# Causal attention on one Trainium2 core: heads in the two row halves of the array, score banks in pairs, one pair of banks and one single bank for the maxima

## The chip, the core and the metric

The program runs on one core of a Trainium2 chip. The core has a matrix engine (TensorE, PE in the profile; its weight loads are PEld), VectorE (DVE), ScalarE (ACT), GpSimd (POOL) and SyncE (SP), which here only issues transfers. The engines run their own instruction streams in order and wait for each other through semaphores. PE reads SBUF and writes PSUM, which has 8 banks of 512 float32 columns on 128 partitions. The metric is the device time of the whole program in microseconds, as a median of several runs.

## The reference, cut to what matters

The program is a chain of eight sub-layers. Two of them are causal attention with 16 heads of 8 channels, on 4 sequences of 1024 tokens, and only those two are touched:

```python
q = q.reshape(B, T, n_head, D)            # B=4, T=1024, n_head=16, D=8
scores = jnp.einsum('bqhd,bkhd->bhqk', q, k) / jnp.sqrt(jnp.float32(D))
causal = jnp.tril(jnp.ones((T, T), dtype=bool))
scores = jnp.where(causal, scores, jnp.float32(-1e+30))
p = jax.nn.softmax(scores, axis=-1)
y = jnp.einsum('bhqk,bkhd->bqhd', p, v).reshape(B, T, C)
return y @ proj_w
```

Everything is float32 in the reference. The kernel keeps that precision for the scores with bfloat16 products: each of q and k is split into three bfloat16 parts, and six products of parts are summed.

## The kernel before

**Inputs.** `causal_inputs` (stage "ci", run as ci0 and ci1) projects eight chunks of 512 tokens, splits q and k into three bfloat16 parts with ACT and DVE, and SP stores the parts of each chunk into the DRAM tensors `q_parts` and `k_parts` (two transfers a chunk, `parts` is double buffered, so ACT waits for a chunk's store two chunks later).

**Attention.** `causal_attention` (stage "ca", run as ca0 and ca1) works on groups: a group G is four heads of one sequence, so there are 16 groups, four to a sequence ("batch"). For each group SP loads a *stack*: `queries` and `keys`, [128, 4 heads, 1024] in bfloat16. Rows 0 to 47 of a stack hold six copies of 8 channels (the six products), rows 64 and 65 hold the shift (minus the row maximum in two bfloat16 parts, against ones in `keys`), and the other rows are zero. Three stacks are used in turn (`RING_CA`). A stack needs 6 transfers for `queries`, 6 for `keys` (8 partitions x 4 heads x 1024 each) and one of zeros. At the start of the stage DVE clears the first stack, POOL the other two, and SP loads each when it is clear.

Two passes run over each group, interleaved:

- *Maxima* (`maximum`, PE L624 and the mask L627, DVE L783): queries against keys with the queries on the partitions, 128 rows by up to 512 keys, masked above the diagonal by a second matmul (identity times a mask), and DVE takes the maximum along the row. `MAXIMA` lists 20 tasks a group. Each task fills one pair of PSUM banks, and two pairs (banks 4-5 and 6-7) are used in turn: PE waits in `next_pair` for the task before the last to be reduced. When all maxima of a group are there, DVE makes the shift (`make_rows`, L792 to L794), PE turns it onto rows (`turn_rows`, L635, also in a pair of banks), ACT copies it out (`copy_rows`, L742) and SP places it into the stack (L564).
- *Scores* (`score`, PE L677 and the mask L680; ACT L759): keys on the partitions, up to 512 queries, for each of 12 units `(qc, kt)` and each of 4 heads one matmul into one of three single banks; ACT raises each bank by itself (exp) into `prob`. `weigh` (PE L691) multiplies `values` with `prob` in float32, four heads side by side in four column strips of 32, into bank 3. Diagonal units (kt >= 4 qc) are narrower (512, 384, 256, 128 columns) and masked: four with qc=0 and four of the eight with qc=1.

The order on PE is written out in the loop over units: score of heads 0 and 1, `between` slot 0, score of heads 2 and 3, `between` slot 1, then `weigh` of the unit before. `BETWEEN` says how many maxima tasks (of the next group) stand in each slot, `ROWS_UNIT` (8) the unit at which the rows are turned, and the tasks after it already belong to the group after the next.

**Batch ends.** When a sequence's four groups are done, `FINISH` puts its closing steps between the units of the next batch's first two groups: `totals` (PE L644: the softmax sums; DVE L800: reciprocal, and L92 to L96: split into bfloat16 parts), four `spread` (PE L654, DVE L809) and two `mix` (PE L662, float32 projection; DVE L819 or L821). The last batch's steps run alone at the end of the stage.

"Local attention" (L1100 to L1337) and the other stages are not touched. They make up the rest of the program.

## Time and profile before

| what | us |
|---|---|
| median of 3 runs | 6053.97 |
| lowest, highest | 6051.51, 6059.97 |
| the profiled execution, its own time | 6055.52 |
| its span, first to last instruction | 6053.7 |
| ca0: first clearing instruction to first matmul | 461.88 to 492.34 |
| ca0: first matmul of the maxima to the last output copy | 492.34 to 1123.4 |
| ca1: first clearing instruction to first matmul | 1686.95 to 1717.59 |
| ca1: first matmul of the maxima to the last output copy | 1717.59 to 2348.79 |

The two causal stages are a fifth of the time. A profile row of a timeline gives the start, the duration, the engine, the line, the operation, what it writes and reads, how many instructions are merged, and in brackets the idle time before it and who ended that. Matmuls are pipelined: a recorded matmul is longer than the time until the next can start, so the step from one start to the next is the price of one. A float32 matmul has two records. "128*32" is the part of the array (rows * columns) that a matmul uses.

### The profile page before, as it was taken

How to read it: one execution, taken by the hardware profiler on the slowest of the kernel's cores; microseconds unless marked ns; L12 is line 12 of the kernel's file. 1: busy time of each engine (PE TensorE's matmuls, PEld its weight loads, DVE VectorE, ACT ScalarE, POOL GpSimd, SP SyncE). 2: the span in 40 equal slices, each digit the busy share in tenths (PEclk: the TensorE clock that was granted, in tenths of full speed). 3: DMA queues.
4: the chain of work that ended last, by engine and by line, in shares of the span. 5: the costliest groups of instructions: out<-in, count | busy, mean ns of one | idle time of the engine just before them, and what ended most of it. 6: DMA issues, size and time to landing. Idle time of an engine off the chain costs nothing. (4 is left out here: it accounts for less than half of the span.)

```text
span 6053.7 us, 164948 instructions
## 1 busy us (share of the span) xinstructions
PE 5119.5 (85%) x72264; PEld 2980.0 (49%) x72592; DVE 4008.1 (66%) x4630; ACT 3245.7 (54%) x4392; POOL 1801.1 (30%) x1232
## 2 busy tenths in 40 slices
PE   6756999788769996998799979997999799979997
PEld 3422333333323332666366636663666366636663
DVE  5756666233366664887488748884888488848884
ACT  2323555322235554776377637763777367736773
POOL 0003000000030001555155515551555055505550
PEclk9988999899889998999899989998999899989998
DMA  0011110000011111111111111110111011101111
GB/s 24 0 48 33 23 23 18 21 0 0 29 39 23 24 21 38 38 38 34 34 39 39 34 33 38 38 38 32 38 38 38 30 37 38 39 31 37 37 37 40
DMA packets 87157, 186.93 MB, mean 31 GB/s; under 512 B 23216, under 2 KB 39088, under 8 KB 84272
## 3 DMA queue, kind: packets, MB, share of 16 engines
q1 hardware_dynamic: 86448, 176.44, 12.1%
q8 instruction: 572, 9.37, 0.6%
q14 instruction: 137, 1.12, 0.1%
HBM read 59.97 MB, written 14.68 MB: 12 GB/s over the span
## 5 line engine op out<-in xcount | busy, mean ns | idle before, releaser
L1327 POOL TENSOR_TENSOR part_of_local<-part_of_local,sine_of_local 128x512 f32<-128x512 f32 x768 | 960.2, 1273 | 1061.3 <-DVE sine_of_local L1264 1061.3
L783 DVE TENSOR_REDUCE top_of_ca<-ps 128x2 f32<-128x1024 f32 (+3 forms) x640 | 695.1, 1115 | 298.6 <-PE ps L627 207.2
L759 ACT ACTIVATE prob_of_ca<-ps 128x512 f32<-128x512 f32 (+3 forms) x1536 | 654.5, 495 | 422.6 <-PE ps L680 311.0
L1334 POOL TENSOR_TENSOR part_of_local<-part_of_local,inverse_of_local 128x1024 f32<-128x1024 f32 x384 | 722.5, 1903 | 139.7 <-DVE inverse_of_local L1296 139.7
L624 PE MATMUL ps<-keys_of_ca,queries_of_ca 128*128 128x512 bf16 (+3 forms) x1474 | 386.4, 332 | 180.6 <-DMA queries_of_ca<-zeros_of_ca 86.4
L1301 DVE TENSOR_REDUCE total_of_local<-prob_of_local 128x16 f32<-128x1024 f32 x192 | 234.3, 1220 | 421.2 <-ACT prob_of_local L1240 421.2
L1261 DVE TENSOR_TENSOR part_of_local<-ps,rope 128x1024 f32<-128x1024 f32 x384 | 466.2, 1214 | 40.7 <-ACT square_of_local L1208 40.7
L1264 DVE TENSOR_TENSOR sine_of_local<-ps,rope 128x1024 f32<-128x1024 f32 x384 | 465.7, 1213 | 0.0
L1100 PE MATMUL ps<-qkv,shifted 128*128 128x512 f32 x768 | 392.4, 635 | 82.1 <-POOL values_of_local L1337 78.5
L1110 PE MATMUL ps<-qkv,shifted 128*128 128x512 f32 x768 | 381.6, 620 | 84.9 <-ACT heads_out_of_local L1236 71.8
L677 PE MATMUL ps<-queries_of_ca,keys_of_ca 128*128 128x512 bf16 (+2 forms) x1464 | 404.0, 331 | 24.3 <-issue 10.8
L1186 PEld LDWEIGHTS ps<-prob_t_of_local,mixed_of_local 64*64 64x64 f32 x12288 | 335.0, 135 | 166.2 <-issue 156.7
L1195 PE MATMUL ps<-heads_out_of_local,wo 128*128 128x128 f32 x3072 | 387.6, 281 | 14.1 <-ACT heads_out_of_local L1236 13.7
L1186 PE MATMUL ps<-prob_t_of_local,mixed_of_local 64*64 64x32 f32 x12288 | 383.8, 221 | 16.0 <-issue 9.1
L1186 PE MATMUL ps<-prob_t_of_local,values_of_local 64*64 64x32 f32 x12288 | 382.0, 219 | 4.7 <-issue 4.2
L1195 PEld LDWEIGHTS ps<-heads_out_of_local,wo 128*128 128x128 f32 x3072 | 368.8, 197 | 16.8 <-ACT heads_out_of_local L1236 16.7
L1167 PE MATMUL ps<-qkv,shifted 128*64 128x512 f32 x1536 | 376.9, 607 | 0.1
L594 POOL MEMSET queries_of_ca<- 32x4096 bf16 x12 | 42.1, 3505 | 1106.1 <-POOLq L63 1105.5
L1226 ACT ACTIVATE keys_of_local<-ps 128x1024 f32<-128x1024 f32 x192 | 196.8, 1025 | 323.2 <-PE ps L1129 323.2
L1247 ACT ACTIVATE values_of_local<-ps 128x1024 f32<-128x1024 f32 x192 | 196.6, 1024 | 306.2 <-PE ps L1167 306.2
L1186 PEld LDWEIGHTS ps<-prob_t_of_local,values_of_local 64*64 64x64 f32 x12288 | 338.0, 135 | 6.8 <-issue 5.9
L691 PE MATMUL ps<-prob_of_ca,values_of_ca 128*32 128x512 f32 (+3 forms) x3072 | 332.5, 505 | 0.0
(207 smaller groups left out, 9928.3 us busy)
## 6 DMA issues: line engine op xcount, KB each, us to landing
mixed_of_local<-values_of_local SPq DMA_DIRECT2D x636, 128.0 KB, 2.4
mixed_of_local<-values_of_local SPq DMA_DIRECT2D x264, 64.0 KB, 2.0
queries_of_ca<-q_parts SPq DMA_DIRECT2D x192, 64.0 KB
keys_of_ca<-k_parts SPq DMA_DIRECT2D x192, 64.0 KB
qkv<-in_qkv SPq DMA_DIRECT2D x7, 1536.0 KB, 6.5
rope<-in_rope SPq DMA_DIRECT2D x7, 1024.0 KB, 9.0
q_parts<-parts_of_ci SPq DMA_DIRECT2D x16, 384.0 KB, 2.5
k_parts<-parts_of_ci SPq DMA_DIRECT2D x16, 384.0 KB, 2.5
```

The lines of the kernel that those rows point to most:

```text
L624: last = nc.tensor.matmul(to[:, h, :], queries[:, first + h, qt * P:(qt + 1) * P], keys[:, first + h, lo:lo + width], start=True, stop=not ...
L677: last = nc.tensor.matmul(to, keys[:, h, kt * P:(kt + 1) * P], queries[:, h, qc * CH + j:(qc + 1) * CH], start=True, stop=not diagonal)
L759: nc.scalar.activation(prob[:, i % 2, h, j:], ps[:, n % SCORE_BANKS, j:], ACT.Exp, scale=scale).then_inc(raised, 1)
L783: nc.vector.reduce_max(top[:, slot, first:first + heads], in_pair(n, heads, width), AX_X)\
L1100: last = nc.tensor.matmul(two_banks(SCORE_SLOT)[:, a, :], xs[:, tokens(t)], w["qkv"][:, 0, chunk(a)], start=True, stop=True)
L1110: last = nc.tensor.matmul(two_banks(KEY_SLOT)[:, a, :], xs[:, tokens(t)], w["qkv"][:, 1, chunk(a)], start=True, stop=True)
L1186: last = nc.tensor.matmul(out, src[rows, t % RING * 2 + i // 2, p + e, :], prob_t[rows, p + e, i * WIN:(i + 1) * WIN], start=True, stop=True)
L1195: last = nc.tensor.matmul(two_banks(OUT_SLOT)[:, 0, 0:P], w["o"][:, p, :], heads_out[:, p, :], start=p == 0, stop=p == PAIRS - 1)
L1261: nc.vector.tensor_tensor(part[:, t % 2, side], by_head(slot), table(2 * side, t), ALU.mult).then_inc(parts, 1)
L1264: nc.vector.tensor_tensor(sine[:, side], by_head(slot), table(2 * side + 1, t), ALU.mult).then_inc(parts, 1)
L1327: nc.gpsimd.tensor_tensor(out, out, sine[:, side, :, (1 - to) * half:(2 - to) * half], ALU.add).then_inc(rotated, 1)
L1334: nc.gpsimd.tensor_tensor(part[:, t % 2, side], part[:, t % 2, side], by, ALU.mult).then_inc(scaled, 1)
```

## The change

The two causal stages only. Constants first: `SHIFT_ROW` goes from 64 to 32, `ROW_HALF` = 64 is new.

- A stack becomes [128, 2, 1024]: of a pair of heads the even one lies in rows 0 to 63 and the odd one in rows 64 to 127 (channels in rows 0-31 and 34-49 of a half, shift in rows 32 and 33, zeros behind). Loads are 12 transfers for `queries`, 12 for `keys` (8 partitions x 2 x 1024) and 2 of zeros, 26 instead of 13.
- The stacks are allocated outside of the stage, cleared by POOL during "ci" (19 chained memsets) and the first three are loaded by SP during "ci", each behind the stores of chunks 3, 4 and 5; "ci" ends when they have landed.
- `score` fills two banks (0-1 or 2-3) with two matmuls of 64 rows each, one in each row half, then the two masks (128 rows). ACT raises two banks with one instruction. The sum bank is 4.
- `maximum`: the 48 pieces (12 strips x 4 heads) are cut into 14 tasks of 4 or 2 pieces in one pair of banks (5-6) and 12 tasks of one piece in a single bank (7), alternating; 26 tasks instead of 20. PE waits for the pair's last task before it fills the pair again, and likewise for the single bank.
- `copy_rows` on ACT moves from within unit 9 to right behind the second exp of unit 8.
- Batch ends: ACT copies the totals out of PSUM, the reciprocal is two halves of 256 columns, the split is two steps, and all steps are spread over units of three groups (11 places instead of 7).

```diff
-MAXIMA = [(qt, lo, width, h, heads, slot) for qt in range(TILES)
-          for lo, width, slot in ([(0, CH, qt)] if qt >= 4 else []) +
-          [(qt // 4 * CH, (qt % 4 + 1) * P, qt + qt // 4 * 4)]
-          for heads in (HG if width <= 2 * P else 2,) for h in range(0, HG, heads)]
+STREAM = [3 * n + 12 for n in range(7)]
+MAXIMA = in_turn([(0, 4), (4, 4), (8, 2)] + [(q, 2) for q in STREAM] + [(32, 4), (36, 4), (40, 2), (44, 2)],
+                 [(10, 1), (11, 1)] + [(q + 2, 1) for q in STREAM[:6]] + [(42, 1), (43, 1), (46, 1), (47, 1)])
-BETWEEN = ((1, 1), (1, 1), (1, 0), (1, 0), (1, 1), (1, 1), (1, 1), (1, 1), (1, 1), (1, 1), (1, 0), (1, 0))
+BETWEEN = ((2, 1), (1, 1), (1, 0), (1, 0), (2, 1), (2, 1), (2, 1), (2, 1), (2, 1), (1, 1), (1, 0), (1, 0))
-FINISH = {(0, 4): ("totals", 0), (0, 6): ("spread", 0), (0, 7): ("spread", 1), (0, 10): ("mix", 0),
-          (1, 4): ("spread", 2), (1, 5): ("spread", 3), (1, 8): ("mix", 1)}
+FINISH = {(0, 4): ("totals", 0), (0, 5): ("invert", 0), (0, 6): ("invert", 1), (0, 7): ("split", 0), (0, 8): ("split", 1),
+          (1, 4): ("spread", 0), (1, 6): ("spread", 1), (1, 8): ("mix", 0),
+          (2, 4): ("spread", 2), (2, 6): ("spread", 3), (2, 8): ("mix", 1)}
...
+                    for low in range(0, pieces, 2):
+                        for n in range(low, min(low + 2, pieces)):
+                            slot, h = divmod(first + n, HG)
+                            qt, lo, width = strip(slot)
+                            diagonal, half = lo + width == (qt + 1) * P, slice(ROW_HALF * (h % 2), ROW_HALF * (h % 2 + 1))
+                            last = nc.tensor.matmul(place_of(n, pieces, width), queries[half, h // 2, qt * P:(qt + 1) * P],
+                                                    keys[half, h // 2, lo:lo + width], start=True, stop=not diagonal)
...
-                        if n >= SCORE_BANKS:
-                            pe.wait_ge(raised, n - SCORE_BANKS + 1)
...
+                    if n >= 2:
+                        pe.wait_ge(raised, n - 1)
+                    for e in range(2):
+                        half = slice(ROW_HALF * e, ROW_HALF * (e + 1))
+                        last = nc.tensor.matmul(ps[:, 2 * two + e, j:], keys[half, two, kt * P:(kt + 1) * P],
+                                                queries[half, two, qc * CH + j:(qc + 1) * CH], start=True, stop=not diagonal)
+                    if diagonal:
+                        for e in range(2):
+                            last = nc.tensor.matmul(ps[:, 2 * two + e, j:j + P], k["ident_b"][:, :], k["after_k"][:, :],
+                                                    start=False, stop=True)
...
-                            nc.scalar.activation(prob[:, i % 2, h, j:], ps[:, n % SCORE_BANKS, j:], ACT.Exp,
-                                                 scale=scale).then_inc(raised, 1)
+                            nc.scalar.activation(prob[:, i % 2, 2 * two:2 * two + 2, j:], ps[:, 2 * two:2 * two + 2, j:],
+                                                 ACT.Exp, scale=scale).then_inc(raised, 1)
...
+                    if 3 <= c < 3 + RING_CA:
+                        if c == 3:
+                            sp.wait_ge(cleared, 1 + 6 * RING_CA)
+                            for slot in range(4):
+                                sp.wait_ge(stored[slot], 16)
+                        load_stack(sp, fetched[c - 3], stacks, zeros, q_parts, k_parts, c - 3)
```

**PE, unit 8 of a group** (the diagonal unit at which the rows are turned; L677, L680 and L691 become L737, L741 and L753, and L624, L627 and L635 become L676, L681 and L689). Before, from the last two scores on:

```order
L677 MATMUL ps<-queries_of_ca,keys_of_ca 128x512
L680 MATMUL ps<-sb_after_k,sb_ident_b 128x128
L677 MATMUL ps<-queries_of_ca,keys_of_ca 128x512
L680 MATMUL ps<-sb_after_k,sb_ident_b 128x128
L635 MATMUL ps<-sb_ident_b,neg_parts_of_ca 8x128 x8
L624 MATMUL ps<-keys_of_ca,queries_of_ca 128x256
L627 MATMUL ps<-sb_after_q,sb_ident_b 128x128
L624 MATMUL ps<-keys_of_ca,queries_of_ca 128x256
```

And after, the whole unit up to its `weigh`:

```order
L737 MATMUL ps<-queries_of_ca,keys_of_ca 128x512 x2
L741 MATMUL ps<-sb_after_k,sb_ident_b 128x128 x2
L676 MATMUL ps<-keys_of_ca,queries_of_ca 128x128 x2
L681 MATMUL ps<-sb_after_q,sb_ident_b 128x128 x2
L676 MATMUL ps<-keys_of_ca,queries_of_ca 128x128 x2
L681 MATMUL ps<-sb_after_q,sb_ident_b 128x128 x2
L676 MATMUL ps<-keys_of_ca,queries_of_ca 128x384
L681 MATMUL ps<-sb_after_q,sb_ident_b 128x128
L737 MATMUL ps<-queries_of_ca,keys_of_ca 128x512 x2
L741 MATMUL ps<-sb_after_k,sb_ident_b 128x128 x2
L689 MATMUL ps<-sb_ident_b,neg_parts_of_ca 8x128 x8
L676 MATMUL ps<-keys_of_ca,queries_of_ca 128x256 x2
```

The matmuls of a pair now stand together, with 64 rows each, and their masks, with 128 rows, behind them; so the part of the array in use changes at each line of the second list. The task behind the turned rows now needs the same pair of banks as these.

**DVE, first group of a batch, units 5 to 8.** Before, the closing steps of the last batch stand in two blocks (the reciprocal and its split at unit 4, a spread at unit 6):

```order
L783 TENSOR_REDUCE top_of_ca<-ps 128x4
L800 RECIPROCAL inverse_of_ca<-ps 128x512
L92 CAST inverse_parts_of_ca<-inverse_of_ca 128x512
L93 SCALAR_TENSOR_TENSOR inverse_of_ca<-inverse_parts_of_ca,sb_minus_first,inverse_of_ca 128x512
L95 CAST inverse_parts_of_ca<-inverse_of_ca 128x512
L96 SCALAR_TENSOR_TENSOR inverse_parts_of_ca<-inverse_parts_of_ca,sb_minus_second,inverse_of_ca 128x512
L783 TENSOR_REDUCE top_of_ca<-ps 128x2 x4
L809 TENSOR_TENSOR evened_of_ca<-summed_of_ca,ps 128x1024
```

After, maxima of pairs (L852, L854) and of single banks (L846) stand between the pieces:

```order
L872 RECIPROCAL inverse_of_ca<-inverse_of_ca 128x256
L846 TENSOR_REDUCE top_of_ca<-ps 128x1
L852 TENSOR_REDUCE top_of_ca<-ps 128x2
L846 TENSOR_REDUCE top_of_ca<-ps 128x1
L872 RECIPROCAL inverse_of_ca<-inverse_of_ca 128x256
L854 TENSOR_REDUCE top_of_ca<-ps 128x2x2
L846 TENSOR_REDUCE top_of_ca<-ps 128x1
L854 TENSOR_REDUCE top_of_ca<-ps 128x2x2
L879 CAST inverse_parts_of_ca<-inverse_of_ca 128x512
L881 SCALAR_TENSOR_TENSOR inverse_of_ca<-inverse_parts_of_ca,sb_minus_first,inverse_of_ca 128x512
L846 TENSOR_REDUCE top_of_ca<-ps 128x1
```

No block of closing steps is left that holds DVE for more than one of them.

**SP, end of "ci".** After, with the stores of chunks 3 to 6:

```order
L505 DMA k_parts<-parts_of_ci 128x3x512
L403 DMA queries_of_ca<-q_parts 8x2x1024 x12
L403 DMA keys_of_ca<-k_parts 8x2x1024 x12
L405 DMA queries_of_ca<-zeros_of_ca 2x2x1024 x2
L505 DMA q_parts<-parts_of_ci 128x3x512
L505 DMA k_parts<-parts_of_ci 128x3x512
L403 DMA queries_of_ca<-q_parts 8x2x1024 x12
```

Before, the stores of all chunks stood in a row there, and the loads stood in "ca" behind the clearing.

## Rows read from the trace of the kernel before

**Rows 1.** The page's head, and its busy time by engine.
```profile
span 6053.7 us, 164948 instructions
...
PE 5119.5 (85%) x72264; PEld 2980.0 (49%) x72592; DVE 4008.1 (66%) x4630; ACT 3245.7 (54%) x4392; POOL 1801.1 (30%) x1232
```

**Rows 2.** Windows: stretch, length, busy (count) by engine, clock, DMA share, GB/s.
```profile
462.00:492.30 30.30, 0.00 (x0) 0.00 (x0) 14.55 (x8) 0.00 (x0) 29.84 (x9) 0.50 0.19 32
...
523.60:1140.00 616.40, 540.49 (x4204) 232.21 (x4271) 377.80 (x385) 355.46 (x816) 5.64 (x14) 0.96 0.12 24
...
1686.00:1717.00 31.00, 0.00 (x0) 0.00 (x0) 14.55 (x8) 0.00 (x0) 29.59 (x9) 0.50 0.18 29
```

**Rows 3.** Windows: a group in the middle, then a batch's first two.
```profile
591.83:624.07 32.24, 30.48 (x261) 13.77 (x264) 22.33 (x24) 22.09 (x52) 0.40 (x1) 1.00 0.16 27
...
656.31:703.87 47.56, 39.95 (x288) 16.34 (x292) 31.27 (x32) 22.67 (x52) 0.40 (x1) 0.93 0.11 18
703.87:742.08 38.21, 35.30 (x273) 15.43 (x276) 25.38 (x27) 22.50 (x52) 0.41 (x2) 1.00 0.13 23
```

**Rows 4.** Timeline, PE and ACT, units 6 to 9 of that group.
```profile
605.47 1.06 PE L691 MATMUL ps<-prob_of_ca,values_of_ca 128*32 128x512 f32 x8
...
607.88 0.38 PE L624 MATMUL ps<-keys_of_ca,queries_of_ca 128*128 128x512 bf16 x1
608.10 0.22 PE L627 MATMUL ps<-sb_after_q,sb_ident_b 128*128 128x128 bf16 x1
608.15 0.38 PE L624 MATMUL ps<-keys_of_ca,queries_of_ca 128*128 128x512 bf16 x1
608.37 0.22 PE L627 MATMUL ps<-sb_after_q,sb_ident_b 128*128 128x128 bf16 x1
608.52 1.07 PE L691 MATMUL ps<-prob_of_ca,values_of_ca 128*32 128x512 f32 x8
609.52 0.39 PE L677 MATMUL ps<-queries_of_ca,keys_of_ca 128*128 128x512 bf16 x1
...
614.27 1.00 ACT L742 ACTIVATE rows_of_ca<-ps 8x1024 bf16<-8x1024 f32 x1
615.33 0.34 PE L624 MATMUL ps<-keys_of_ca,queries_of_ca 128*128 128x384 bf16 x1 [1.26 <-ACT rows_of_ca L742]
```

**Rows 5.** Timeline, PE in local attention, where row halves are used.
```profile
3004.44 2.00 PE L1156 MATMUL ps<-keys_of_local,queries_of_local 64*32 64x64 f32 x128
3006.37 1.94 PE L1167 MATMUL ps<-qkv,shifted 128*64 128x512 f32 x8
```

**Rows 6.** Groups by line and shape: count, busy us, mean ns, idle before.
```profile
L783 DVE TENSOR_REDUCE top_of_ca<-ps 128x2 f32<-128x1024 f32 x384 | 457.4, 1221 | 142.0 <-PE ps L624 81.5 <-PE ps L627 56.0
L759 ACT ACTIVATE prob_of_ca<-ps 128x512 f32<-128x512 f32 x768 | 402.4, 604 | 204.2 <-PE ps L680 101.1 <-PE ps L677 69.0 <-remote 34.0
...
L783 DVE TENSOR_REDUCE top_of_ca<-ps 128x4 f32<-128x512 f32 x64 | 44.2, 691 | 30.0 <-PE ps L627 27.3 <-DVE neg_parts_of_ca L794 0.3
```

**Rows 7.** The page's group of an ACT instruction over two banks.
```profile
L1226 ACT ACTIVATE keys_of_local<-ps 128x1024 f32<-128x1024 f32 x192 | 196.8, 1025 | 323.2 <-PE ps L1129 323.2
```

**Rows 8.** Timeline, the starts of ca0 and ca1.
```profile
461.88 3.50 POOL L594 MEMSET queries_of_ca<- 32x4096 bf16 x1 [461.42 <-POOLq L63]
...
480.43 2.04 SPq L556 DMA_DIRECT2D queries_of_ca<-q_parts  x6
...
492.34 0.29 PE L624 MATMUL ps<-keys_of_ca,queries_of_ca 128*128 128x128 bf16 x1 [44.69 <-DMA queries_of_ca<-zeros_of_ca]
...
1683.49 0.36 SPq L469 DMA_DIRECT2D k_parts<-parts_of_ci  x1
...
1717.59 0.29 PE L624 MATMUL ps<-keys_of_ca,queries_of_ca 128*128 128x128 bf16 x1 [41.70 <-DMA queries_of_ca<-zeros_of_ca]
```

**Rows 9.** Timeline, DVE in a batch end and at ca1's end.
```profile
665.36 3.36 DVE L800 RECIPROCAL inverse_of_ca<-ps 128x512 f32<-128x512 f32 x1 [1.99 <-PE ps L644]
...
2330.71 2.59 DVE L809 TENSOR_TENSOR evened_of_ca<-summed_of_ca,ps 128x1024 f32<-128x1024 f32 x2 [1.25 <-PE ps L654]
```

More of the change, by code:

```diff
@@ L629, in maximum @@
-                    last.then_inc(ready, 1)
+                    if i == 0 and G >= RING_CA:
+                        pe.wait_ge(loaded[G % RING_CA], STACK_LOADS * (G // RING_CA))
+                    if pieces > 1:
+                        take_pair()
+                    else:
+                        take_lone()
+                    for low in range(0, pieces, 2):
[5 more added lines that the diff above has]
+                                                    keys[half, h // 2, lo:lo + width], start=True, stop=not diagonal)
+                        for n in range(low, min(low + 2, pieces)):
+                            qt, lo, width = strip((first + n) // HG)
+                            if lo + width == (qt + 1) * P:
+                                last = nc.tensor.matmul(place_of(n, pieces, width)[:, width - P:], k["ident_b"][:, :],
+                                                        k["after_q"][:, :], start=False, stop=True)
@@ L667, in score, with finish @@
+                def finish(b, step, which):
+                    if step == "totals":
+                        totals(b)
+                    elif step == "spread":
+                        spread(b, which)
+                    elif step == "mix":
+                        mix(b, which)
+                def score(G, i, two):
                     qc, kt, j = UNITS[i]
                     queries, keys = stacks[G % RING_CA]
-                    diagonal = kt >= 4 * qc
-                    if i == 0 and heads[0] == 0:
+                    diagonal, n = kt >= 4 * qc, 2 * (G * NU + i) + two
+                    if i == 0 and two == 0:
@@ L717, in _ @@
                     G, i = divmod(u, NU)
-                    score(G, i, (0, 1))
-                    between(G, i, 0)
-                    score(G, i, (2, 3))
-                    between(G, i, 1)
+                    for two in range(2):
+                        score(G, i, two)
+                        between(G, i, two)
                     if u:
@@ L771, in _ @@
                 sum_out(ALL - 1, 1)
+                take_totals(lones)
                 act.wait_ge(acc_out, 2 * ALL)
@@ L850, in _ @@
                 maximum(NM)
-                next(task)
+                next(pairs)
                 for m in range(NM + 1, NM + AHEAD):
```

349 lines of the change are left out of this document (184 added, 165 removed).

## The prediction, made before the changed kernel ran

> **What bounds the kernel now.** I read the page's head first: the span is 6053.7 us, and PE is the busiest engine at 85% of it [rows 1]. Only the two causal stages change, so I went on to windows over them [rows 2]. Each has a start in which PE does nothing at all (30.3 us in ca0, 31.0 in ca1: DVE and POOL clear stacks, then a load lands) and a long body in which PE is busy 540 of 616 us. The body repeats itself, so I took one group of it: 32.24 us, PE 30.48 busy, DVE 22.33, ACT 22.09, clock 1.00 [rows 3]. PE bounds the group. The two other windows there are the groups that carry a batch end: 47.56 and 38.21 us, so a batch end costs 15.3 + 6.0 = 21.3 us, part of it at a lower clock (0.93).
>
> Then I priced PE by the steps between starts [rows 4]. A 512-column bfloat16 matmul takes 607.88 to 608.10, 0.216 us. Its 128-column mask takes 608.10 to 608.15, 0.055. The float32 weighing begins 0.15 behind the last mask (608.37 to 608.52) and the next score starts 1.00 behind it (608.52 to 609.52); streaming is 2048 column passes at 2.4 GHz, 0.85. So going from the full array to 32-column strips costs about 0.095 beyond the matmul itself, and going back about as much again. The unit 605.47 to 608.52 checks these prices: 1.00 + 0.095 + 8 x 0.216 + 4 x 0.055 = 3.04 against 3.05 measured. By them a group is 9.4 us of scores (18,432 columns and 32 masks), 9.4 of maxima, 7.7 of weighing, 0.45 of turned rows and 26 changes of array shape at 0.095 (2.5): 29.5, and with small overheads 29.8. The other 2.4 us are waits, 1.26 of them one wait for ACT's copy of the rows.
>
> **The change, part by part. (a) The start.** The clearing and the first load leave the stage: 461.9 to 492.3 in ca0 and 1687.0 to 1717.6 in ca1 [rows 8], 30.4 + 30.6 = 61.0 us. They go under "ci", where POOL is idle; its 3.50 us memset of 32x4096 halves with its size, so 19 chained ones take about 33 us. SP gets three loads of 26 transfers: at 2.04 us for six [rows 8] one load takes 26 x 0.34 = 8.8 us to issue, ahead of the next chunk's stores. The first load of before (13 transfers, the same bytes) was ready 11.9 us after its first issue (480.43 to 492.34); twice as many, half as long transfers may take between that and twice that. In ci0 three loads from about 420 on end near 462, when the stage ends anyway: 0 to 4 us lost, I take 2. In ci1 the stage is shorter: clearing ends near 1661, the loads follow, the stores of chunks 4 and 5 stand behind them, ACT waits for these two chunks later, and the stage then ends 9 to 20 us behind its last store of before (1683.5), I take 14, nearer to the load's measured 11.9. Net: -61 + 16 = -45 us.
>
> **(b) PE's work in a group.** If the two halves of a pair run side by side, a score pair costs 0.216 instead of 0.43: -3.8 us. Of the 48 maxima pieces 36 are paired and 12 stand alone, so their columns fall from 18,432 to 12,032: -2.7. Masks stay. Against that, a pair uses 64 rows, its mask 128, the weighing 32-column strips: I counted 88 changes of shape in the order of a group where there were 26. The trace has no change between the full array and full-width halves. The nearest rows are those in [rows 4] and one in local attention, where 64*32 matmuls give way to 128*64 ones: all are about 0.095. I take that: 62 x 0.095 = +5.9. The bounds are 0 and, for a full pipeline, 0.16 (0.38 recorded against 0.216 stepped). PE's work is then 29.8 - 6.5 + 5.9 = 29.2 us, hardly less than before. That halves overlap isn't proved by the trace: the 128 records of L1156 in eight array parts take 1.93 us (3004.44 to 3006.37) [rows 5], against 6.8 us one after the other, but 1.7 us if only the four column strips overlapped. So a pair costs between 0.22 and 0.43, and I take 0.22, since column strips do overlap (8 records of mean 605 ns in 1.06 us).
>
> The Trainium skill, "TensorE: Matmul & The Clock Gate", section "Packing small matmuls", says that matmuls in different row groups run concurrently (four of 32 rows 3.07 times as fast); [rows 5] doesn't contradict it. The skill's "TensorEngine Tiling (Array Packing)", "Key Properties", says that changing the tiling mode drains the array. That speaks against this change, and the 0.095 in [rows 4] agrees. By the first page alone the body would gain 6.5 us a group, 28 x 6.5 = 182 us.
>
> **(c) The waits in a group.** Times by [rows 6] and [rows 7]: a reduction of 1024 columns 1.22 us, of 512 0.69; exp over two banks 1.03 instead of 2 x 0.60; the rows' copy 1.00; a release reaches PE 0.06 later (615.27 to 615.33), a result its reader about 0.2 after the last start. DVE's sum grows by six instructions of 0.16 to 23.3, ACT's falls to about 20. Neither is the bound over a group, but both are over parts of it. I walked through the group in PE's order, from unit 4, where three maxima tasks (2, 1, 2 banks) stand in each unit:
> - unit 4: DVE has 3.1 us of work, PE 1.5. PE fills the pair, the single bank, scores, then must wait until the first pair is reduced: 1.0 us.
> - unit 5: the same for its pair: 0.6.
> - unit 6: 0.1.
> - unit 7: two pair tasks follow each other, with a 0.96 us reduction between: 1.0.
> - unit 8: turned rows and the next task use the same pair. ACT first ends the second exp of the unit (1.03), then copies (1.00): 1.65 against 1.26 + 0.2 before. Queued behind this wait on PE are the weighing of unit 7 and all of unit 9.
> - the rest: 0.1. Here PE is the bound with 15.7 us up to the next unit 4.
> Together 4.5 us, so a group takes 29.2 + 4.5 = 33.7 us against 32.24: +1.45. For 14 groups of each stage: 28 x 1.45 = +41 us.
>
> **(d) The last two groups** of a stage have few or no maxima. There the exps over two banks leave fewer waits between ACT and PE: -4.5 a stage, -9.
>
> **(e) Batch ends.** The first group pays 1.9 for totals on PE and the rest by DVE's 3.4 us of reciprocal [rows 9] and 2.4 of split in units where DVE is already late: 5.5. The next two pay a spread twice (2.1 each) and a float32 mix of 3.5 on PE less some overlap: 7.3 each. Sum 20.1 against 21.3: six batch ends, -7. The serial end of a stage gets a copy of the totals (0.6 and a handover) and no longer fills the second pair while DVE reads the first (2.59 for two in a row [rows 9]): +2.5 a stage, +5.
>
> **Sum:** -45 + 41 - 9 - 7 + 5 = -15 us. The profiled execution took 6055.52 (span 6053.7 and 1.8 around it), so it would become 6040.5; the median of before is 1.55 lower, so the median of after is about **6039 us**, 0.25% less.
>
> **Rivals.**
> - *Change of shape is cheap* between full array and row halves (0 to 0.03 us). PE's work falls to about 24.7, DVE holds units 4 to 7 (12.4 us), the rest shrinks by some 4: about 30 us a group, 28 x -3.7 = -104: near 5935. For it: no row shows this very change. Against: every other change of shape that I found costs the same. The page's promise of twice the speed for pairs is this case.
> - *Slower: the hand-over of the single pair is the bound.* In each group five waits of PE (c) end on one reduction or copy, where before two pairs took turns and PE could be a task ahead. If each is 0.3 us longer than my walk, or the loads of 26 transfers come late for the group after the next, a group is 35.2: +42, near 6081. It decides against the kernel from 34.2 us a group on (28 x 0.5 = 14 more uses up the gain). For it: DVE's work in units 4 to 7 is already 10.9 us against PE's 10.3.
> - *The halves don't overlap* (the change doesn't do what it says): PE's work +6.5, of which perhaps 5 shows: 28 x 5 = +140, near 6179.
> - *The loads choke "ci":* transfers at half the rate, stores queued behind: 22 us more, near 6061.
> - *The walk is too strict* by 0.8 us a group, since tasks of both kinds can run ahead a little: -22, near 6017.
>
> **How the numbers follow.** Forecast 0.50 (own range 6020 to 6060), cheap change 0.10, slower by the hand-over 0.18, no overlap 0.06, loads 0.05, walk too strict 0.11. The range leaves out the cheap change, no overlap and the far ends of the others: 5990 to 6095. A measurement of this kernel can tell 0.2%, 12 us, from no change, so faster means below 6042 and slower above 6066: faster 0.10 + 0.11 + 0.28 of the forecast's half = 0.49; same 0.17 + 0.03 = 0.20; slower 0.31.
>
> **What the profile of after would show.** (a) The first matmul of ca0 within 1 us of the stage's start, the end of ci1 later by some 14 us than its last store before. (b) In a diagonal score 0.31 us from the first L737 to the first L741, and two L737 starts a few ns apart; with 0.22 the cheap change holds, with 0.5 there is no overlap. (c) POOL's copies of values 33.7 us apart in the middle of a batch; waits of PE's L676 on DVE and on ACT's copy of the rows of about 4.5 us a group. (e) About 20 us more in three groups of a batch, at clock 1.00. I am wrong if the distance in the middle of a batch is under 33 or over 34.5 us.

## The result, and the profile of the changed kernel

The changed kernel takes **6147.7 us** (median of four runs, 6133 to 6152), the kernel before beside it 6054.0. The ratio is 1.0142, with a 95% interval of 1.0123 to 1.0160: slower by some 86 us by the ratio, and 94 between the two medians. The forecast was 6039 with a range of 5990 to 6095, so both the sign and the range were wrong.

The page's head and windows over the changed kernel answer to [rows 1] and [rows 3]. The columns of a window are as in [rows 2]: stretch, length, busy time of PE, PEld, DVE, ACT and POOL, clock, DMA share, GB/s.

```profile
span 6147.5 us, 164154 instructions
...
PE 5202.0 (85%) x72386; PEld 2892.2 (47%) x72592; DVE 4000.2 (65%) x4814; ACT 3214.3 (52%) x3632; POOL 1770.4 (29%) x1242
```
```profile
465.67:546.14 80.47, 65.46 (x397) 20.13 (x397) 53.43 (x67) 24.79 (x30) 2.30 (x4) 0.69 0.01 4
...
580.79:616.85 36.06, 32.51 (x266) 10.80 (x264) 22.92 (x30) 21.01 (x28) 0.40 (x2) 0.95 0.10 26
...
616.85:651.50 34.65, 31.11 (x266) 10.70 (x264) 22.93 (x30) 21.02 (x28) 0.41 (x2) 1.00 0.09 24
651.50:692.87 41.37, 34.81 (x282) 11.24 (x280) 28.20 (x36) 21.84 (x29) 0.40 (x2) 0.96 0.08 21
692.87:736.66 43.79, 37.39 (x277) 12.48 (x276) 26.05 (x33) 21.12 (x28) 0.40 (x2) 0.96 0.08 19
736.66:780.40 43.74, 37.30 (x277) 12.48 (x276) 26.05 (x33) 21.11 (x28) 0.40 (x1) 0.96 0.07 20
856.45:904.03 47.58, 41.25 (x277) 12.77 (x276) 26.12 (x33) 21.12 (x28) 0.40 (x2) 0.86 0.07 18
```

The first row is the prologue (maxima of group 0, PE's work ahead of the first score) with group 0 in ca0, from the first matmul on. The third row is a quiet group: 34.65 us, where [rows 3] has 32.24 and the forecast 33.7. The second is the same group with its clock at half speed (1.2 instead of 2.4 GHz) for a part. The next three are one batch end in three groups, each with such a fall (0.96), and the last is one of them where the clock fell longer.

Added up over the two stages, from one profiled execution each (6149.3 against 6055.5 us):

| stretch | forecast | measured |
|---|---|---|
| (a) both starts, "ci" with them | -45 | -46.6 |
| prologue and group 0, both stages | +3 (as two groups) | +27.1 |
| (b, c) 26 quiet groups, 34.65 - 32.24 each | +38 | +62.7 |
| (e) six batch ends, 20.4 at full clock against 21.3 | -7 | -5 |
| falls to half clock inside the groups | 0 | +46 |
| (d) last two groups of a stage | -9 | -8 |
| serial ends | +5 | +3 |
| stages that the change doesn't touch | 0 | +15 |

A fall costs 1.4 us or more: 36.06 - 34.65. What the batch ends take without it is read below from "full_rows", where some stand at clock 1.00. The falls are what is left of 98.5 us, by which both stages grew behind group 0, when the rows for quiet groups, batch ends, last groups and serial ends are taken off. The last row can't be called an effect of the change: between profiled executions these stages differ that much with the same code. Behind ca1 the kernel before takes 3705.6 us and the changed kernel 3717.9, but of the kernels below "early_before" takes 3729.1, "own_masks_three" 3721.0 and "filled_prologue" 3704.4.

**The start** did what the sum said. Timeline of the changed kernel, PE in both stages and SP at the end of "ci1":

```profile
465.67 0.29 PE L676 MATMUL ps<-keys_of_ca,queries_of_ca 64*128 64x128 bf16 x2 [14.11 <-PEq L65]
...
1690.55 4.04 SPq L403 DMA_DIRECT2D queries_of_ca<-q_parts  x12
1694.63 4.05 SPq L403 DMA_DIRECT2D keys_of_ca<-k_parts  x12
1698.73 1.41 SPq L405 DMA_DIRECT2D queries_of_ca<-zeros_of_ca  x2
...
1724.90 1.10 SPq L505 DMA_DIRECT2D k_parts<-parts_of_ci  x1
...
1730.41 0.29 PE L676 MATMUL ps<-keys_of_ca,queries_of_ca 64*128 64x128 bf16 x2 [20.26 <-PEq L65]
```

This load holds SP for 9.6 us (1690.55 to 1700.14, estimated 8.8), the next two for 10.5 each. The stores of the next chunk stand behind each of them. From the first matmul of "ci1" to the start of ca1 it now takes 14.5 us longer (estimated 14), and in "ci0" the same time as before. So the two idle starts of 61.1 us less 14.5 give the 46.6.

**The quiet group.** Its timeline on PE, units 4, 5, 7 and 8:

```profile
624.53 0.39 PE L676 MATMUL ps<-keys_of_ca,queries_of_ca 64*128 64x512 bf16 x2 [0.89 <-DVE top_of_ca L852]
...
626.26 0.39 PE L676 MATMUL ps<-keys_of_ca,queries_of_ca 64*128 64x512 bf16 x2 [0.34 <-DVE top_of_ca L852]
...
634.25 0.39 PE L676 MATMUL ps<-keys_of_ca,queries_of_ca 64*128 64x512 bf16 x2 [0.84 <-DVE top_of_ca L852]
...
635.79 0.39 PE L737 MATMUL ps<-queries_of_ca,keys_of_ca 64*128 64x512 bf16 x2
636.11 0.28 PE L741 MATMUL ps<-sb_after_k,sb_ident_b 128*128 128x128 bf16 x2
636.33 0.23 PE L676 MATMUL ps<-keys_of_ca,queries_of_ca 64*128 64x128 bf16 x2
...
640.13 0.28 PE L676 MATMUL ps<-keys_of_ca,queries_of_ca 64*128 64x256 bf16 x2 [1.47 <-ACT rows_of_ca L787]
```

The four waits of the walk are all there, in the units it named: 0.89, 0.34, 0.84, 1.47 against 1.0, 0.6, 1.0, 1.65. And a score pair gives way to its mask after 0.32 us (635.79 to 636.11): 0.216 for two matmuls side by side and 0.10 for the change of shape. Overlap and price were right. What was wrong is found below.

### The profile page after: what moved, and what is told of

Same layout as the page of the kernel before. It is cut to its first block and busy times, and to the rows that moved or that the text cites. A ratio compares the mean times of both kernels' runs of the same rounds, so it can differ in the third digit from the quotient of the medians.

```text
span 6147.5 us, 164154 instructions
## 1 busy us (share of the span) xinstructions
PE 5202.0 (85%) x72386; PEld 2892.2 (47%) x72592; DVE 4000.2 (65%) x4814; ACT 3214.3 (52%) x3632; POOL 1770.4 (29%) x1242
## 5 line engine op out<-in xcount | busy, mean ns | idle before, releaser
L814 ACT ACTIVATE prob_of_ca<-ps 128x1024 f32<-128x1024 f32 (+3 forms) x768 | 615.7, 812 | 564.1 <-PE ps L741 394.4
L676 PE MATMUL ps<-keys_of_ca,queries_of_ca 64*128 64x512 bf16 (+3 forms) x1536 | 342.3, 355 | 201.6 <-DVE top_of_ca L852 77.4
L852 DVE TENSOR_REDUCE top_of_ca<-ps 128x2 f32<-128x1024 f32 (+1 forms) x320 | 374.0, 1169 | 140.0 <-PE ps L681 84.8
L1275 PE MATMUL ps<-heads_out_of_local,wo 128*128 128x128 f32 x3072 | 388.9, 281 | 13.8 <-ACT heads_out_of_local L1316 13.5
L637 POOL COPY values_of_ca<-vtok 128x256 f32<-128x256 f32 x32 | 12.7, 402 | 1200.8 <-PE ps L753 1200.7
L753 PE MATMUL ps<-prob_of_ca,values_of_ca 128*32 128x512 f32 (+3 forms) x3072 | 355.1, 536 | 0.4 <-ACT summed_of_ca L800 0.4
L1327 ACT ACTIVATE values_of_local<-ps 128x1024 f32<-128x1024 f32 x192 | 196.6, 1024 | 303.4 <-PE ps L1247 303.4
L846 DVE TENSOR_REDUCE top_of_ca<-ps 128x1 f32<-128x512 f32 (+1 forms) x384 | 245.8, 640 | 132.5 <-PE ps L681 97.3
```

Of the source, the lines that this page charges most:

```text
L753: last = nc.tensor.matmul(ps[h * QUAD:(h + 1) * QUAD, SUM_BANK, j:], values[:, G % 2, kt, h, :], prob[:, i % 2, h, j:], start=kt == 0, sto ...
L814: nc.scalar.activation(prob[:, i % 2, 2 * two:2 * two + 2, j:], ps[:, 2 * two:2 * two + 2, j:], ACT.Exp, scale=scale).then_inc(raised, 1)
L852: nc.vector.reduce_max(to, pair[:, :, 0:width], AX_X).then_inc(pair_used, 1)
L1275: last = nc.tensor.matmul(two_banks(OUT_SLOT)[:, 0, 0:P], w["o"][:, p, :], heads_out[:, p, :], start=p == 0, stop=p == PAIRS - 1)
```

## The experiments

Ratios are to the kernel before, run on the same chip. In all, the question is which of four things made the groups and the prologue longer: the changes of shape, the row halves themselves, the changed banks and order, or the clock.

**1. The early loads alone.** First the kernel before, with its stacks of 128 rows, cleared and loaded early (cut to the lines that matter):

```
-                sp.wait_ge(first_cleared, 8)
-                load(0)
+    (in "ci", behind the stores of chunks 3, 4, 5)
+                        load_stack(sp, fetched[c - 3], stacks, zeros, q_parts, k_parts, c - 3)
```

> The kernel before with one part of the change alone: the stacks (still one of 128 rows with four heads, 13 transfers a load) are cleared by POOL in the stages ahead and the first three loads go out under "ci". Theory (step (a) of the prediction is right, and the cold prologue of the changed kernel comes from its row halves): the first matmul of ca0 and ca1 comes 27 to 30 us sooner, the clock rises some 5 us behind the first matmul as in the kernel before, the first group ends 67 us behind the first matmul as before: 45 to 55 us less than before, about 6003. Rival (the clock stays low because PE starts right behind the stage "ci"): the prologues take about 80 us instead of 67, and only 20 to 28 us are gained, about 6030. In both the distance in the middle of a batch stays 32.24.

Measured: 0.9985 (0.9974 to 0.9996). Neither theory had it: the memsets for two stacks were longer than the layernorm that I had put them under, and "ci0" began 29 us late. That is a fault of the experiment, mended in the next.

> As "early_before", but the clearing no longer fills the layernorms ahead: there one stack is cleared (24.5 us), under "ci" two, two loads go out under "ci" and the third in the attention stage. In "early_before" the stage "ci0" began at 410.9 instead of 381.6 us and ca0's first matmul stood where it had stood before, since 49 us of memsets are longer than a layernorm. Theory (step (a) holds for the full array): "ci0" begins within 3 us of before, both stages' first matmuls come 25 to 30 us sooner, "ci1" ends 0 to 8 us later than before; in all 45 to 55 us less than before. Rival (the early loads cost under "ci" or in the prologue what they save): less than 20 us.

Measured: **0.9925** (0.9900 to 0.9950), 46 us less. The first matmuls come 30.3 us (ca0) and, from the start of "ci1", 28.7 us (ca1) sooner, and the distance in the middle stays 32.24. Step (a) is confirmed apart from the rest. With the loads of the changed kernel put back into the attention stages:

> The changed kernel with clearing and the first three loads back in the attention stages. Theory (row halves keep the clock low whatever came before; step (a) of the prediction holds): PE's first matmul comes about 24 us behind the stage's start, "ci1" ends 13 us sooner, the prologue stays at clock 0.50 for its whole length: 25 to 35 us slower than the changed kernel. Rival (the clock stayed low because the start was early): the prologue is at full clock 5 us behind the first matmul and 13 us shorter in each stage, so that the time is within 10 us of the changed kernel.

Measured: 1.0194 (1.0177 to 1.0212), 31 us slower than the changed kernel, as the theory said. The prologue of ca0 takes 79.06 us at a mean clock of 0.71; it was 80.47 at 0.69 in the changed kernel. That isn't the 0.50 throughout that I had expected, but it shows that the early start doesn't cause the slow prologue.

**2. Without the changes of shape.** Each mask now goes into its head's row half, by two matmuls of 64 rows; constants with swapped halves are added (put in short, as it is for the even head):

```
-  nc.tensor.matmul(to, k["ident_b"][:, :], k["after_k"][:, :], start=False, stop=True)
+  own = slice(ROW_HALF * e, ROW_HALF * (e + 1))
+  nc.tensor.matmul(to[:, low], k["ident_b"][own, :], k["after_k"][own, low], start=False, stop=False)
+  nc.tensor.matmul(to[:, high], k["ident_r"][own, :], k["after_k_r"][own, high], start=False, stop=True)
```

> The changed kernel, but each causal mask is added by two matmuls of 64 rows in the half of its head (the constants stand a second time with their halves swapped; 128 and 64 columns), so that scores, maxima and masks have one shape and only weighing and turned rows change it: 26 changes of shape a group instead of 88. Theory (a change of shape costs 0.095 us on PE and PE bounds much of the group): 5.9 us less PE work; part of it turns into waits for DVE in units 4 to 7, so the quiet group falls from 34.65 to 30.5 to 31.5 us and the whole by 85 to 120 us, to 6030 to 6060. Rival (the hand-over of the single pair is the bound, changes of shape lie beside it): the group stays above 33.8 and the whole falls by less than 25 us.

Measured: **0.9853** (0.9836 to 0.9869), 175 us less than the changed kernel, more than I had expected. The quiet group:

```profile
595.14:624.49 29.35, 25.01 (x330) 10.71 (x328) 22.79 (x30) 20.45 (x28) 0.41 (x2) 1.00 0.10 29
```

62 changes of shape fewer (26 instead of 88) take 5.3 us off a group, 0.085 each: most of their 0.10 lay on the path. The rest of the gain is in prologue and batch ends, and in the falls of the clock: no quiet group of this kernel shows one.

**3. Without the overlap.** Both heads of a pair use row half 0, so the second head gets the wrong rows:

> The changed kernel, but both heads of a pair use the first row half (the second head reads the first one's rows, so its results are the wrong head's): same instructions, shapes and banks, no overlap. Theory 1 (the halves do run side by side): PE's work in a group rises by 3.8 us of scores and 2.7 of maxima, the quiet group from 34.65 to 39 to 41 us, the whole by 110 to 170 us. Theory 2 on the clock (it stays low in the prologue because of how long PE works, not because of the rows used): the prologue's matmuls now keep PE busy twice as long and the clock rises within 20 us as in the kernel before. Rival to 2 (64 rows are too few whatever the time): it stays at 0.50 for the whole prologue, which gets longer still.

Measured: 1.1488 (1.1454 to 1.1522). One pair at full clock, then a quiet group:

```profile
722.93 0.60 PE L737 MATMUL ps<-queries_of_ca,keys_of_ca 64*128 64x512 bf16 x2
723.47 0.28 PE L741 MATMUL ps<-sb_after_k,sb_ident_b 128*128 128x128 bf16 x2
```
```profile
576.34:642.19 65.85, 64.62 (x265) 15.74 (x264) 23.69 (x30) 21.56 (x28) 0.40 (x2) 0.50 0.05 12
```

The pair takes 0.54 instead of 0.32 us, so the halves of the changed kernel do run side by side. But the group was not 39 to 41 us. The clock is 0.50 for the whole prologue of ca0 (116 us) and 0.56 on average over the 554 us behind it; in the group shown it stays at half speed while PE is busy for 64.6 of 65.9 us. My theory on the clock falls, its rival holds.

**4. The waits for DVE, and the batch ends.** DVE's maxima over half the columns of each piece; and the changed kernel without the batch ends inside the stages:

> The changed kernel with each of DVE's maxima taken over half the columns of its piece (the shift is then only a part's maximum). Theory (2.1 us of a quiet group are waits of PE for DVE through the single pair of banks, the rest is PE's own work and the copy of the rows): the quiet group falls from 34.65 to 32.3 to 32.8 us, batch ends by as much, the whole by 55 to 75 us. Rival (DVE is the bound over a longer stretch, PE only seems busy): the group falls below 31.5. Other rival (the waits move to ACT's exp): above 34.

> The changed kernel without the batch ends inside the two stages: the totals, inverses, spreading and mixing of the first three batches are left out, only the last batch's at the stage's end are made. Theory (a batch end costs 25 us at full clock, and the waits in it bring most of the clock falls): six batch ends, 150 us, and 10 to 20 us of falls go: 150 to 175 us less than the changed kernel. Rival (the falls come from the quiet groups' own waits and changes of shape): only 140 to 150 us, and 3.4 us at half clock still stand in every second or third group. By step (e) of the prediction it would be 120.

Windows of quiet groups, one of "half_reduce", then one of "no_batch_ends":

```profile
531.83:566.34 34.51, 32.35 (x266) 10.81 (x264) 13.96 (x30) 20.77 (x28) 0.40 (x1) 0.95 0.09 24
```
```profile
549.04:586.46 37.42, 33.87 (x266) 10.89 (x264) 22.92 (x30) 20.99 (x28) 0.40 (x1) 0.91 0.07 21
```

"half_reduce": 0.9996 (0.9984 to 1.0009), 88 us less than the changed kernel. The waits for DVE in a group fell from 2.1 to 0.7 us, yet the group stayed at 34.5. Every one now had a part at half clock (0.95), and a fall costs the 1.4 us that the waits had given back. The theory (32.3 to 32.8) missed this, and so did the rival that named 34, since no wait for an exp appeared. The gain came from batch ends and prologues. The prologue of ca0 shows DVE's share in it, at a clock as low as the changed kernel's:

```profile
460.55:531.83 71.28, 64.25 (x397) 19.96 (x397) 32.54 (x68) 24.56 (x30) 2.30 (x5) 0.70 0.02 4
```

"no_batch_ends": 0.9879 (0.9856 to 0.9901), 159 us less. That is the 120 us by which step (e) had it, and falls of the clock: 26 groups now take 14 us more than 26 x 34.65, where some 46 had been lost. So my 25 us a batch end were 20 of work and 5 of clock, and falls stay in groups without any batch end, up to 37.42 us, as the rival said.

**5. Full rows in the changed order.** The changed kernel's banks, tasks, exps and batch ends, but stacks of 128 rows (and the third load in the attention stage):

```
-  queries[half, h // 2, qt * P:(qt + 1) * P], keys[half, h // 2, lo:lo + width]
+  queries[:, h, qt * P:(qt + 1) * P], keys[:, h, lo:lo + width]
```

> The changed kernel with its order of tasks, its pair and single bank, its exps over two banks, its spread batch ends and early loads (two under "ci", the third in the attention stage), but with stacks of 128 rows and four heads, loads of 13 transfers, as in the kernel before: no row halves. Theory (the row halves are what costs: 61 changes of shape a group and a clock that 64-row matmuls do not raise): the prologue to the end of the first group takes 64 to 68 us instead of 80, the clock falls go, the quiet group is 32 to 33 us, and the whole is 6000 to 6035. Rival (the hand-over through one pair and one single bank is what costs): the quiet group stays above 34 us and the whole above 6060.

Measured: 1.0076 (1.0055 to 1.0097), 6102 us. My theory falls. Its quiet group, its first batch end with the first group of the next, and PE's waits in the quiet group show why:

```profile
582.60:617.06 34.46, 31.32 (x265) 14.16 (x264) 23.03 (x30) 21.03 (x28) 0.40 (x1) 1.00 0.16 25
```
```profile
651.52:691.35 39.83, 33.63 (x281) 14.34 (x280) 28.31 (x36) 21.75 (x29) 0.41 (x2) 1.00 0.13 21
691.35:733.73 42.38, 36.12 (x277) 15.88 (x276) 26.16 (x33) 21.03 (x28) 0.41 (x2) 1.00 0.13 21
733.73:776.11 42.38, 36.12 (x277) 15.88 (x276) 26.16 (x33) 21.03 (x28) 0.40 (x2) 1.00 0.12 20
810.57:851.91 41.34, 35.14 (x281) 14.71 (x280) 28.29 (x36) 21.74 (x29) 0.40 (x1) 0.96 0.13 20
```
```profile
PE ps L678 <- DVE top_of_ca L854: 1.7, 3, 0.8
PE ps L678 <- ACT rows_of_ca L789: 1.3, 1, 1.3
```

The group is 2.2 us longer than before with the same matmuls: three new waits of PE for DVE through the single pair of banks. A batch end at clock 1.00 is 5.4 + 7.9 + 7.9 = 21.2 us here, and one fall to 0.96 costs 1.5 (41.34 against 39.83). Taking that 1.5 off the changed kernel's 41.37, 43.79 and 43.74 leaves 5.2 + 7.6 + 7.6 = 20.4. "late_loads", whose groups have the changed kernel's code, has one such group at clock 1.00, the second of a batch end's three. It is 7.7 above 34.65:

```profile
1037.58:1079.94 42.36, 35.92 (x277) 12.40 (x276) 26.06 (x33) 21.12 (x28) 0.41 (x2) 1.00 0.06 16
```

The cross test keeps the row halves and goes back to the banks, order and batch ends of before:

> The kernel before's banks and order (two pairs of banks for maxima in turn, three single score banks, one exp a head, its batch ends), with the change's row halves (masks in the full array as in the change) and early loads. Theory (the row halves are nearly even, -6.5 for overlap and +6 for changes of shape, and the single pair of the change costs its 2.2 us a group): the quiet group is 31.4 to 32.3 us, 2.3 to 3.2 below the change's 34.65, and the whole 5985 to 6020, near "early_before_two". Rival (row halves need the change's order, since a pair of scores now waits for two of three banks): above 33.5. For the clock: if 64-row matmuls keep it low, the prologue shows 45 us or more at half clock as in the change; if the gaps of the single pair do, 20 us or less, as in the kernel before.

> "two_pairs_full_masks" with each mask in the row half of its head, as in "own_half_masks": before's banks and order, row halves, 26 changes of shape a group. Theory (with changes of shape and hand-over both gone, PE's own work of 24.1 us and the 1.5 us wait for the rows remain, and ACT's 22.1 and DVE's 22.3 us come close): quiet group 26 to 28.5 us, the whole 5840 to 5900, below every kernel so far. Rival (ACT becomes the bound, since 48 exps of one bank each wait for scores that come in pairs): quiet group 29 us or more, no better than "own_masks_three".

Measured: 1.0015 (1.0003 to 1.0026) and **0.9828** (0.9811 to 0.9845). Neither side of the first expectation had it: its group takes 33.35 us, between 32.3 and 33.5. Windows of prologue with group 0, and of a quiet group, for "early_before_two", "full_rows" (prologue), "two_pairs_full_masks" and "halves_two_pairs":

```profile
462.07:525.91 63.84, 51.89 (x391) 23.58 (x398) 50.94 (x54) 25.98 (x57) 2.30 (x4) 0.96 0.11 17
558.15:590.39 32.24, 30.48 (x261) 13.77 (x264) 22.34 (x24) 22.08 (x52) 0.41 (x2) 1.00 0.17 26
```
```profile
468.41:548.14 79.73, 61.94 (x396) 27.45 (x397) 53.18 (x67) 24.59 (x30) 2.30 (x5) 0.75 0.08 14
```
```profile
461.64:530.96 69.32, 59.73 (x398) 18.73 (x398) 51.98 (x54) 26.07 (x56) 2.30 (x5) 0.72 0.05 16
530.96:564.31 33.35, 30.94 (x266) 10.52 (x264) 22.55 (x24) 22.26 (x52) 0.40 (x2) 1.00 0.09 25
```
```profile
466.62:527.93 61.31, 48.39 (x513) 20.37 (x514) 51.35 (x54) 25.92 (x56) 2.29 (x4) 0.73 0.07 18
527.93:557.70 29.77, 25.80 (x329) 10.60 (x330) 22.32 (x24) 22.27 (x52) 0.40 (x2) 1.00 0.09 28
```

Together they make a table of the quiet group (in brackets prologue with group 0, ca0):

| | banks and order of before | of the change |
|---|---|---|
| full rows | 32.24 (63.8) | 34.46 (79.7) |
| row halves, masks full | 33.35 (69.3) | 34.65 (80.5) |
| row halves, masks in them | 29.77 (61.3) | 29.35 (69.4) |

Read down, row halves cost a group 1.1 us or next to nothing while the masks change the shape, and save 2.5 to 5.1 when they don't. Read across, the changed banks and order cost 2.2 us with full rows, 1.3 with row halves, and nothing in the last line. The effects don't add up: "halves_two_pairs" got 29.77 instead of 26 to 28.5, because scores now wait for ACT's exps, as its rival had said (PE's waits, over 557.70 to 587.59):

```profile
PE ps L719 <- ACT prob_of_ca L806: 2.3, 7, 0.6
PE ps L662 <- ACT rows_of_ca L789: 1.5, 1, 1.5
```

In the prologue the changed banks and order cost 16, 11 and 8 us, the lower clock that came with them included.

**6. The clock in the prologue.** Full-array matmuls of no use behind each of the 33 tasks ahead of the first score (the expectation says 31); they write a score bank:

> The changed kernel with two more matmuls of the full array (512 columns, bfloat16, result not used) behind each of the 31 tasks of maxima ahead of the first score. Theory (the clock stays at half speed for 58 us because 64-row matmuls with gaps keep too little of the array at work, and this costs the prologue 13 us): the clock is full within 10 us, and first matmul to end of the first group falls from 80 to about 70 us in both stages: 15 to 25 us less in all. Rival (something else holds the clock down): it stays at 0.50, the 62 matmuls cost 0.43 us each, and the time rises by 20 to 50 us.

Measured: 1.0104 (1.0087 to 1.0121), 23 us less than the changed kernel. That is the expected size, but by luck. The clock does come up (window over prologue and group 0 of ca1, below; 0.86 in ca0), yet the window shrinks from 81.2 to 75.2 in ca1 and from 80.5 to 79.9 in ca0: 6.5 us of the 27, with the time of the added matmuls in it. The two profiled executions are 14.1 us apart, and 13.5 of them lie behind ca1, in stages that the edit doesn't touch. So 6.5 us is what this experiment shows.

```profile
1743.48:1818.69 75.21, 68.77 (x459) 22.46 (x463) 52.88 (x67) 24.62 (x30) 2.30 (x5) 0.95 0.02 4
```

**7. A version that beats both.** "own_half_masks" with four more edits, in three steps. First the third load goes out in the attention stage and the spreading moves, then one task of maxima moves, last the prologue is filled. The two tables, in short:

```
-  (2, 1), (2, 1), (2, 1), (2, 1), (2, 1), (1, 1), (1, 0), (1, 0))      tasks between scores, units 4 to 11
+  (2, 1), (2, 1), (2, 1), (2, 1), (2, 0), (2, 1), (1, 0), (1, 0))
-  (1, 4): ("spread", 0), (1, 6): ("spread", 1)        first slot of the unit
+  (1, 2): ("spread", 0), (1, 3): ("spread", 1)        second slot
```

> "own_half_masks" with two more edits: the third load goes out in the attention stage instead of under "ci", and in a batch end the two pairs of totals are spread in the second slot of units 2 and 3, where no task of maxima follows at once. Theory: "ci1" ends 7 to 10 us sooner; of the 2.6 us that PE waits for the spreading in each of two groups of a batch end, 1.5 to 2.5 go, 12 such groups, 18 to 30 us: in all 25 to 40 us less than "own_half_masks". Rival (the spreading holds up the tasks behind it wherever it stands, since DVE's work is the same): only the 7 to 10 us of the load.

> "own_masks_two" with one task of maxima moved from behind the turned rows in unit 8 to unit 9, so that PE does not need the pair of banks while ACT ends an exp and copies the rows (1.1 to 1.5 us in each group). Theory: that wait goes in 30 groups, 25 to 40 us less than "own_masks_two". Rival (the tasks behind it are late by as much, since DVE and the single pair are the bound there): less than 10 us.

> "own_masks_three" with one more full-array matmul of 512 columns (result not used) behind each of the 31 tasks of maxima ahead of the first score. Theory (64-row matmuls alone do not raise the clock, full-array ones do): the time at half clock in the prologue falls from about 50 to below 20 us and each prologue becomes 4 to 7 us shorter: 8 to 14 us less. Rival: the clock rises, but the added matmuls cost what it gives back, or it does not rise: within 5 us or slower.

Measured: 0.9830 (0.9803 to 0.9857), **0.9771** (0.9752 to 0.9791) and 0.9762 (0.9733 to 0.9792). By the ratios the first step gave 14 us where 25 to 40 were expected, nearer to its rival's 7 to 10, and the second 36, within its 25 to 40. The third load outside "ci1" brings ca1's first matmul 6 us nearer to the start of "ci1". In a batch-end group the waits for the spreading are 0.5 us, where the changed kernel has 2.6, but 1.4 of it came back as a wait for the reduction ahead. Moving one task behind the turned rows took the wait for ACT away, and the quiet group fell only from 29.33 to 28.99, since PE now waits for DVE instead; batch ends gained more (36.04 a group instead of 36.4 to 37.8). The filled prologue adds nothing that can be told from zero: ca1's goes from 68.4 to 66.6 us at clock 0.87, ca0's from 68.0 to 71.4. The best version takes some 5924 us where the kernel before took 6061.

## Where the prediction was right, and which steps failed

**(a) Right.** -46.6 against -45, with both parts of it (starts, SP's queue in "ci1"). The rival "loads choke" is out.

**(b) Overlap and price of a change of shape: right.** 0.22 for a pair, 0.10 for a change. The Trainium skill's "TensorEngine Tiling (Array Packing)", "Key Properties", says that changing the tiling mode drains the array. That was the rule that spoke against this change, and the trace agrees: with 62 such changes fewer a group is 5.3 us shorter. The rivals "change is cheap" and "the halves don't overlap" are out. The net saving of PE's work was near too: 29.8 - 29.2 = 0.6 by the forecast, and 0.4 by the next point's 30.8 for full rows and 30.4 for row halves.

**What failed in (b)** is the sentence "The other 2.4 us are waits". It took 29.8 for PE's own work of before. But the waits of that group are 1.26 us for ACT, and each wait costs some 0.17 more than its idle, since the idle is counted from the recorded end of the last matmul (0.38 behind its start, where the next could start after 0.216). So the work was 32.24 - 1.4 = 30.8. "full_rows" says the same: 34.46, less 3.0, less four times 0.17, is 30.8, and the changed kernel has 34.65 - 3.54 - 0.7 = 30.4. The forecast began 1 us too low, which is the difference of 33.7 and 34.65, and 25 us in all. Some 0.6 of it can be read in [rows 4]. The way back from 32-column strips was priced like the way there, 0.095, but the next score starts 1.00 behind the weighing, 0.15 more than the 0.85 of streaming. Twelve weighings a group make 12 x 0.05 = 0.6. The rest isn't located.

**(c) Right, place by place.** 3.5 us of idle in four waits, 4.2 with the 0.17 of each, against 4.5. The rival "walk too strict" is out. The rival "the single pair is the bound" had the mechanism that "full_rows" isolates; I gave it 0.18 because I priced it only as an error on top of the walk. By "full_rows" it is 2.2 of the 2.4 us that a quiet group lost.

**The prologue had no term.** The sum priced 28 groups, and took the time from the first matmul to the first score as unchanged. There 26 tasks of group 0 and seven of group 1 stand behind one another with hardly anything between them, so that the hand-over of the banks is paid again and again. Without the 2 x 2.4 us of the two groups this omission is 22 of the 27 us. "full_rows" puts 16 us a stage on the changed banks and order. "half_reduce" took 9 us off ca0's prologue with the clock as low as before (0.70 against 0.69), which speaks for the hand-over. Raising the clock gave 6.5 us net in both stages together. How the 22 us split between the two isn't shown.

**(e) Right at full clock**: 5.2 + 7.6 + 7.6 = 20.4 us against 5.5 + 7.3 + 7.3. Timeline of the changed kernel, PE in such a group:

```profile
706.51 0.60 PE L707 MATMUL ps<-inverse_parts_of_ca,sb_spread_total 128*128 128x512 bf16 x2
708.43 0.23 PE L676 MATMUL ps<-keys_of_ca,queries_of_ca 64*128 64x128 bf16 x2 [1.31 <-DVE evened_of_ca L889]
...
710.99 1.94 PE L753 MATMUL ps<-prob_of_ca,values_of_ca 128*32 128x512 f32 x8
...
717.74 3.65 PE L715 MATMUL ps<-evened_of_ca,sb_cproj 128*128 128x512 f32 x8
721.33 0.23 PE L676 MATMUL ps<-keys_of_ca,queries_of_ca 64*128 64x128 bf16 x2
```

A spread holds PE for 1.92 us (706.51 to 708.43; priced 2.1), the mix for 3.6. The clock falls 2 to 3 us behind the wait for the spreading: the weighing at 710.99 takes 1.94 us instead of the 1.07 of [rows 4].

**The clock had no term.** The prediction asked for batch ends "at clock 1.00", and gave no group a fall. The falls inside groups are some 46 us, the largest item of the miss: without them the changed kernel would take some 6100, about as "full_rows" does.

(d) and the serial ends were right within 2 us each.

## What to carry to other kernels

Price the stretch in which nothing hides a hand-over, the prologue, by itself, before multiplying the steady group. When the summed steps (29.8 us here) and the waits that the trace shows (1.4) don't reach the group's length (32.24), look for the rest in the prices before calling it a wait. And when a packing into row or column tiles saves time only between changes of shape, look first at whether the small matmuls in between (here the masks) can be brought into the same tiles: that turned 1.4% slower into 1.5% faster. Where PE is the bound the clock needs a term of its own, and the granted clock is to be read group by group, since a stage's mean hides the falls.

## What the runs showed of the chip that I had not expected

- PE being busy did not by itself bring the clock up. In "one_half", with scores and maxima in 64-row matmuls one after the other, PE was busy 64.6 of 65.9 us, and the clock stayed at 1.2 GHz. In the kernel before it rose behind the stretch below, 4.9 us in which PE was busy for 4.2 with full rows:

```profile
492.34:497.20 4.86, 4.20 (x24) 2.79 (x26) 2.93 (x4) 0.00 (x0) 4.80 (x2) 0.50 0.54 94
```

- Full rows alone don't hold it up either: in the prologue of "full_rows" the mean is 0.75 over 79.7 us. Each of two edits took that mean down from the 0.96 of "early_before_two": the changed banks and order (0.75), and the row halves with the banks and order of before (0.72, and 0.73 with the masks in the halves). Why isn't shown.
- Falls to half clock inside quiet groups stood in kernels with 81 to 88 changes of shape a group (the changed kernel, "half_reduce", "no_batch_ends", "filled_prologue", "late_loads", "two_pairs_full_masks", 1.4 to 2.8 us each), and in those with 26 only in three groups of "own_masks_two". Shorter waits didn't keep them away: "half_reduce" had one in every quiet group and lost to the clock what it had gained there. Why they fall in one group and not in the next stays open.
